# A gated-attention and mixture-of-experts layer on one core: the relative bias split into a constant on ScalarE and a short matmul part

## What is computed

```
qk  = einsum('bis,bjs->bij', q, k)
idx = arange(L)[None, :] - arange(L)[:, None] + (L - 1)        # L = 512
qk  = qk + w_rel[idx][None]                                    # w_rel has 2*128 - 1 = 255 entries
kernel = square(relu(qk / sqrt_s))
out = u * einsum('bij,bje->bie', kernel, v)
```

## Time and profile before

| | |
|---|---|
| median of 3 runs | 356.28 us (356.17 to 356.88) |
| profiled execution, its time | 356.23 us |
| profiled execution, its span | 354.2 us (2.0 us lie around it) |
| granted clock of PE, mean | 0.976 |
| PE / ACT / DVE / POOL busy | 89% / 68% / 67% / 54% of the span |
| attention stage, ticks a = 0 to 7 | about 34 to 198 us |
| expert blocks | about 201 to 341 us |

### The profile page before, as it was taken

How to read it: one execution, slowest core, us unless ns; L and a number is a source line. 1 busy time by engine, 2 the same in 40 slices (tenths; PEclk the granted TensorE clock), 3 DMA queues, 4 the chain that set the end, 5 groups by cost and what they waited for, 6 DMA issues and landing times.

```text
span 354.2 us, 7616 instructions
## 1 busy us (share of the span) xinstructions
PE 314.9 (89%) x2031; PEld 255.1 (72%) x2031; DVE 238.2 (67%) x739; ACT 239.5 (68%) x466; POOL 190.0 (54%) x193
## 2 busy tenths in 40 slices
PE   1279999999999999999996879999999999999940
PEld 1167657575756647575653779999999999999940
DVE  1578548888787778879869466785555555556843
ACT  1455948969798796979654348677777777776710
POOL 7150305136667586647658077657776455455460
PEclk9999999999999999999999699999999999999995
DMA  6983100000101010010101232323333322239518
GB/s 161 306 296 88 44 0 2 0 0 24 39 8 45 10 38 23 25 38 8 55 15 46 60 94 68 93 70 85 106 103 99 95 71 74 61 81 332 164 41 237
DMA packets 33403, 28.39 MB, mean 80 GB/s; under 512 B 5399, under 2 KB 28868, under 8 KB 33364
## 3 DMA queue, kind: packets, MB, share of 16 engines
q1 hardware_dynamic: 25634, 16.43, 16.6%
q0 software_dynamic: 4320, 8.47, 7.2%
q10 hardware_dynamic: 3410, 3.03, 3.2%
HBM read 16.75 MB, written 11.61 MB: 80 GB/s over the span
## 4 chain that ended last, share of the span: by engine, by line
PE 49%; POOL 12%; issue 12%; DVE 11%; ACT 11%; DMA 3%; SPq 1%; POOLq 0%; ACTq 0%; DVEq 0%
PE B_o L855 17%; PE B_uv L844 17%; POOL slots L455 6%; PE B_o L794 4%; ACT xs L540 2%; PE B_m L718 2%; ACT gswap L582 2%; ACT acc L540 2%; ACT s_rel L564 2%; PE B_o L785 2%; POOL rs L446 1%; DVE go L1045 1%; PE B_S L769 1%; ACT gbase L576 1%; ACT th_u L525 1%
## 5 line engine op out<-in xcount | busy, mean ns | idle before, releaser
L486 POOL DMA_INDIRECT y<-u,xb x71 | 70.4, 992 | 47.6 <-ACT u L654 37.1
L855 PE MATMUL B_o<-W2s,K 128*128 x568 | 75.3, 276 | 2.3 <-DVE K L1203 2.3
L455 POOL DMA_INDIRECT slots<-rows,pos x64 | 64.8, 1013 | 18.6 <-issue 17.3
L855 PEld LDWEIGHTS B_o<-W2s,K 128*128 128x128 f32 x568 | 69.0, 192 | 2.8 <-issue 2.7
L785 PE MATMUL B_o<-K,v 128*128 128x512 f32 x128 | 59.3, 596 | 0.0
L643 ACT ACTIVATE t<-W1s 128x644 f32 x36 | 26.6, 740 | 21.9 <-DVE yd L1209 21.3
L844 PE MATMUL B_uv<-xbT,t 128*128 128x128 f32 x288 | 38.1, 275 | 0.0
L1203 DVE TENSOR_TENSOR K<-B_uv,t 128x512 f32<-128x512 f32 x36 | 24.8, 692 | 18.4 <-PE B_uv L844 18.2
L785 PEld LDWEIGHTS B_o<-K,v 128*128 128x128 f32 x128 | 22.9, 190 | 19.8 <-issue 18.2
L844 PEld LDWEIGHTS B_uv<-xbT,t 128*128 128x128 f32 x288 | 35.1, 192 | 0.0
L773 PE MATMUL B_S<-G,ident_r 128*128 128x512 f32 x64 | 32.9, 594 | 0.0
(11 more groups left out here) (197 smaller groups left out, 653.4 us busy)
## 6 DMA issues: line engine op xcount, KB each, us to landing
xb<-slots SPq DMA_DIRECT2D x71, 65.0 KB, 1.9
x_all<-L_attn_x SPq DMA_DIRECT2D x8, 256.0 KB, 3.1
W1s<-L_ffn_W SPq DMA_DIRECT2D x1, 2048.0 KB, 11.7
x_all<-y SPq DMA_DIRECT2D x4, 512.0 KB, 6.4
out<-acc SPq DMA_DIRECT2D x6, 256.0 KB
y<-u,xb POOLq DMA_INDIRECT x71, 2.3
slots<-rows,pos POOLq DMA_INDIRECT x64, 2.4
slots<-zrow SPq DMA_DIRECT2D x9, 65.0 KB, 2.9
```

What stands on the lines that cost most here:

```text
L455: pool.indirect_dma_start(out=slots, out_offset=bass.IndirectOffsetOnAxis(ap=pos[:, q % 2, c:c + 1], axis=0), in_=rows[:, q % 2, c // T, c ...
L486: pool.indirect_dma_start(out=y2, out_offset=bass.IndirectOffsetOnAxis(ap=xb[:, k, D:D + 1].bitcast(u32), axis=0), in_=yb[:, k, :], in_off ...
L855: last = nc.tensor.matmul(B_y[n % 2], hT[:, n % 2, c * P:(c + 1) * P], W2s[:, bass.ds(w + c * D, D)], start=(c == 0), stop=(c == T - 1))
```

## The change

Three things are done. Relu takes the last entry of w_rel as a bias, one value for all partitions, read through an SBUF operand `w_last` that a new DMA on ACT's queue fills. `G` holds the bias minus that constant, 256 columns wide, and the bias matmuls run for j-tile 0 on its last 256 columns and for j-tile 1 on its last 128 alone. Everything that builds `G` shrinks accordingly: 384 entries in `w_row` and `w_long`, 256 columns in `w_skew`, two blocks in PE's `bias_window`. ACT waits for the new DMA in batch 0 and DVE in its `bias_window`. Per tick this takes 8 bias matmuls of 512 columns to 2 of 256 and 2 of 128.

```diff
--- before.py
+++ after.py
@@ -53,7 +53,7 @@
 
     slots = nc.dram_tensor("slots", [SLOTS, RW], f32).ap()
     y2 = nc.dram_tensor("y2", [ROWS * TOPK, D], f32).ap()
-    w_long = nc.dram_tensor("w_long", [1, 2 * L - 1], f32).ap()
+    w_long = nc.dram_tensor("w_long", [1, 3 * P], f32).ap()
     NREL = w_rel.shape[1]
 
     ctx = ExitStack()
@@ -93,7 +93,8 @@
         uvT = sb("uvT", [P, 2, 5 * P], f32r)
         owT = sb("owT", [P, 2, D])
 
-        G = sb("G", [P, 2, 7 * P], f32r)
+        G = sb("G", [P, 2, 2 * P], f32r)
+        w_last = sb("w_last", [P, 1])
         ident_r = sb("ident_r", [P, P], f32r)
         gb = sb("gb", [P, 2, 2])
         g_half = sb("g_half", [P, 2])
@@ -141,12 +142,12 @@
         gswap = sb("gswap", [P, 2, L])
         t1 = sb("t1", [P, 2, L])
 
-        w_row = th_u[0:1, 0:2 * L - 1]
+        w_row = th_u[0:1, 0:3 * P]
 
         t2 = sb("t2", [P, 2, L])
         qk = sb("qk", [P, 2, L])
         s_rel = sb("s_rel", [P, 2, L])
-        w_skew = s_rel[:, :, :].rearrange("p k l -> p (k l)")[:, 0:7 * P]
+        w_skew = s_rel[:, :, :].rearrange("p k l -> p (k l)")[:, 0:2 * P]
         K = sb("K", [P, T, L])
         go = sb("go", [P, 2, L])
         x1 = sb("x1", [P, T, D])
@@ -221,7 +222,7 @@
         s_ld_uvw, s_ld_b1, s_ld_small, s_ld_skew = sem("uvw_loaded"), sem("b1_loaded"), sem("small_loaded"), sem("skew_loaded")
         s_w_row, s_ld_rope, s_ld_rep, s_ld_w1 = sem("bias_row_filled"), sem("rope_loaded"), sem("rep_loaded"), sem("w1_loaded")
         s_ld_w2, s_ld_b2 = sem("w2_loaded"), sem("b2_loaded")
-        s_ld_affine = sem("ffn_affine_loaded")
+        s_ld_affine, s_ld_last = sem("ffn_affine_loaded"), sem("last_bias_loaded")
         s_pool0 = sem("pool_constants")
         s_wT_ps, s_wT = sem("weights_transposed_psum"), sem("weights_transposed")
         s_gh = sem("g_half_ready")
@@ -332,7 +333,7 @@
             sp.dma_start(sinT[:, :], rope_sin).then_inc(s_ld_rope, 16)
             sp.wait_ge(s_ld_skew, 32)
             sp.dma_start(w_skew[:, :], bass.AP(tensor=w_long.tensor, offset=0,
-                                               ap=[[1, P], [1, 7 * P]])).then_inc(s_ld_skew, 16)
+                                               ap=[[1, P], [1, 2 * P]])).then_inc(s_ld_skew, 16)
             for rep, vector in ((res_rep, res_scale), (br_rep, br)):
                 sp.dma_start(rep[:, :], vector.partition_broadcast(P)).then_inc(s_ld_rep, 16)
             load_x(2)
@@ -498,6 +499,8 @@
         def _(act):
             act.dma_start(w_row[:, 0:NREL], w_rel).then_inc(s_ld_skew, 16)
             act.dma_start(ow_raw[:, :], o_w).then_inc(s_ld_uvw, 16)
+            with nc.allow_non_contiguous_dma(reason="one word for all partitions, once"):
+                act.dma_start(w_last[:, :], w_rel[0, NREL - 1:NREL].partition_broadcast(P)).then_inc(s_ld_last, 16)
             with nc.allow_non_contiguous_dma(reason="512 words, once"):
                 for n, w in enumerate((gamma, beta)):
                     act.dma_start(gb[:, n, :], w.rearrange("k s -> s k")).then_inc(s_ld_small, 16)
@@ -561,7 +564,8 @@
 
                 act.wait_ge(s_ps, 4 * b + j + 1)
                 after(act, k_step, 8 * b + 2 * j - 2)
-                nc.scalar.activation(s_rel[:, j % 2, :], B_S[:, j % 2, :], ACT.Relu).then_inc(k_step, 1)
+                after(act, s_ld_last, 0 if b else 16)
+                nc.scalar.activation(s_rel[:, j % 2, :], B_S[:, j % 2, :], ACT.Relu, bias=w_last[:, :]).then_inc(k_step, 1)
                 if j == 0:
                     after(act, av_ps, b)
                 act.wait_ge(k_step, 8 * b + 2 * j + 1)
@@ -701,8 +705,8 @@
 
 
                 te.wait_ge(s_ld_skew, 48)
-                for s in range(7):
-                    d = 6 - s
+                for s in range(2):
+                    d = 1 - s
                     last = nc.tensor.matmul(B_o[:, s * P:(s + 1) * P], w_skew[:, d * P:(d + 1) * P], flip[:, :],
                                             start=True, stop=True)
                 last.then_inc(s_wT_ps, 1)
@@ -766,12 +770,13 @@
                 for j in range(T):
                     if not isinstance(b, int) or 4 * b + j >= 2:
                         te.wait_ge(k_step, 8 * b + 2 * j - 3)
-                    nc.tensor.matmul(B_S[:, j % 2, :], qk[:, 1, j * P:(j + 1) * P], qk[:, 0, :],
-                                     start=True, stop=False)
-
-                    for part in range(2):
-                        last = nc.tensor.matmul(B_S[:, j % 2, :], ident_r[:, :], G[:, part, (3 - j) * P:(3 - j) * P + L],
-                                                start=False, stop=(part == 1))
+                    varies = (2 - j) * P
+                    last = nc.tensor.matmul(B_S[:, j % 2, :], qk[:, 1, j * P:(j + 1) * P], qk[:, 0, :],
+                                            start=True, stop=True)
+                    if varies > 0:
+                        for part in range(2):
+                            last = nc.tensor.matmul(B_S[:, j % 2, L - varies:], ident_r[:, :], G[:, part, 0:varies],
+                                                    start=False, stop=(part == 1), skip_group_check=True)
                     last.then_inc(s_ps, 1)
 
             def attend(b, q, tiles):
@@ -945,7 +950,7 @@
             ts(selcum[:, :], ones[:, 0:NE], 0.0, None, ALU.mult).then_inc(s_dve0, 1)
 
             dve.wait_ge(s_ld_skew, 16)
-            cp(w_row[:, NREL:], w_row[:, NREL - 1:NREL].broadcast_to([1, 2 * L - 1 - NREL])).then_inc(s_w_row, 1)
+            cp(w_row[:, NREL:], w_row[:, NREL - 1:NREL].broadcast_to([1, 3 * P - NREL])).then_inc(s_w_row, 1)
 
             def small_weights():
                 dve.wait_ge(s_ld_small, 16 * 4)
@@ -972,9 +977,11 @@
             def bias_window():
                 dve.wait_ge(s_wT_ps, 2)
                 cp(ident_r[:, :], ident[:, :])
-                cp(G[:, 0, :], B_o[:, 0:7 * P]).then_inc(s_wT, 1)
+                dve.wait_ge(s_ld_last, 16)
+                ts(G[:, 0, :], B_o[:, 0:2 * P], w_last[:, :], None, ALU.subtract).then_inc(s_wT, 1)
                 dve.wait_ge(s_wT, 3)
-                tt(G[:, 1, :], B_o[:, 0:7 * P], G[:, 0, :].bitcast(f32), ALU.subtract).then_inc(s_wT, 1)
+                stt(G[:, 1, :], B_o[:, 0:2 * P], w_last[:, :], G[:, 0, :].bitcast(f32), ALU.subtract,
+                    ALU.subtract).then_inc(s_wT, 1)
 
             def ln1_stats(b):
                 link = chain(ln1_step, 3, b)
```

## The result

The changed kernel takes 360.50 us (median of 4 runs, 359.46 to 362.07) against 356.47 for the kernel before; the ratio is 1.0116, with an interval of 1.0074 to 1.0158. Measured once more on another chip it was 1.0119 (1.0083 to 1.0155), at a median of 360.84 us against 356.26. One of its six runs, 364.44 us, lies over 1.5% above its fastest; it is in that median and not in the ratio. The prediction had 357.1 us and a range up to 358.0. The direction held, the size did not: over three quarters of the loss of 4.0 us lies outside the sum of +0.9.

A forecast was written before the change was run, and what follows sets the result against it. The prediction took ACT and DVE to set the tick period, with PE close behind. Its terms, -0.30 + 0.06 + 0.04 + 0.93 + 0.2 = +0.9 us on 356.23, gave 357.1 us, range 355.4 to 358.0.

The forecast's parts named there:

- What bounds a tick: Attention ticks: ACT and DVE set the period of 20.6 us, PE is close behind, no scores matmul in the chain.
- rival 3: Attention ticks: PE was the bound after all, 1.37 us fall away in each of 7 periods, 346.6 us; chance 0.07.
- Part 2: Relu's bias operand on ACT: 0.19 us more on the period, +0.93 us over ticks 2 to 6.
- d: Extra ACT time of one Relu for its SBUF operand: taken as 93 ns, bounds 0 and 191 ns.
- rival 1: Relu on ACT: the operand is free where ACT waits anyway, d near 0, 355.5 us; chance 0.17.
- Part 3: Opening: DVE's copy filling the row shrinks from 0.45 to 0.15 us, -0.30 us; the new DMA costs nothing.
- Part 5: Ticks 0 and 1: earlier starts on ACT against four operand costs each, +0.06 and +0.04 us.
- Part 6: The end: output(7) runs at the low clock and the clock's return comes later, +0.2 us, bounds 0 and 0.3.
- Part 4: Building G in the opening: less work costs nothing, though PE then idles about 2.7 us before project_v(0).
- rival 2: Opening: the clock falls in the new gap before project_v(0), +1.5 us, 358.6 us; chance 0.08.
- Part 1: Bias matmuls in each tick: PE relieved of 1.37 us, worth nothing in the period as PE waits longer for xs.

The follow-up runs named there:

- alone-run: Changed kernel with PE's matmuls and the opening put back as in the kernel before, so only Relu's operand is new: 357.76 us, ratio 1.0038.
- e6: Kernel before with only G built the short way, scores unchanged, PE's gap before project_v(0) left open: repeat 356.71 us, ratio 1.0014.
- e7: Kernel before with G built the short way plus five unread blocks in bias_window filling PE's gap: repeat 355.20 us, ratio 0.9973.

## Why the prediction was wrong

**What bounds a tick: right.** The chain runs through ACT and DVE, and no scores matmul is in it. The period is 20.78 us for a predicted 20.8, and rival 3 is out.

**Part 2, the operand: right.** d was taken as 93 ns; the runs with none, one and two give about 90 and 86. The alone-run, which the account put at 358.0 (nothing starts earlier there), took 357.8. The changed kernel itself has 674 ns, 85 more. The point from which rival 1 decides, 41 ns, is far off.

**Part 3: right,** 0.33 us for 0.30, and the new DMA is nowhere in a chain. **Part 5: right,** ticks 0 and 1 together moved by -0.02 us for the +0.10 forecast. **Part 6: right,** 3.37 us for output(7), +0.2 as said; PE had been idle 4.18 us before the first block's transpose. The blocks' first B_o<-W2s,K starts another 0.1 us later that no term has.

**Part 4, the lost cover: the first failed step.** The gap of 2.55 us was weighed between one of 1.86 that did no harm and one of almost 3.5 that did, and the sum took the harmless side, with 0.08 for rival 2. The clock fell there in all six profiles with the short build and no filling, after gaps of 2.09 to 2.88 us, and in none with a gap of 1.92 or less. In the run with the short matmuls alone it fell 1.2 us after project_v(0) had begun. Rival 2's 1.5 us is what it cost (1.54 in the trace, 1.5 between the medians of e6 and e7). The prediction also misread its citation: the warning of the Trainium skill, page TensorE: Matmul & The Clock Gate, section "Why this matters for your kernels", is for gaps somewhat longer than this one, so it did not put the cost of rival 2 into the sum. What decides here are the traces: the clock at 0.50 from 24 us on.

**Part 1, "in the period this is worth nothing, since PE only waits longer for xs": the second failed step,** and one that no rival covered. The size was right: from the start of the scores to that of project_u PE takes 3.90 us in tick 4 (118.24 to 122.14) for 5.29 before (116.69 to 121.98), 1.39 less for the 1.37 forecast. The split of a j-tile behind that forecast, 0.86 us for q and k and 0.46 for the bias matmuls, does not come out of the starts in the earlier trace rows, which would give 0.46 and 0.86; it stands in the chain of waits (0.86 at 37.07 us, 0.46 at 37.92), and the 1.39 bears it out. The edit was costed at nothing with ACT as the cover, but the bias matmuls had themselves kept up the clock. The work taken from PE became 0.9 to 1.24 us of idle time before the router, and the 0.48 before the transposes stayed, with only eight matmuls of 8 columns in between; the prediction had expected one wait of 1.9 us for xs. In ticks where the clock then fell, attend of the last tile and the first part of project_v ran at half the rate behind xs, where PE has nearly no slack, and such a tick lost 1.1 to 1.4 us. I weighed idle time and clock for the one long gap and not for the ticks. The profiles show one or two such falls between 40 and 190 us. The median stands 3.4 us above the sum, and 1.9 above the sum with rival 2 in it (358.6).

With both terms the sum is 357.1 + 1.5 = 358.6, and with one or two falls in the ticks at 1.4 each 360.0 to 361.4; the measurement is 360.5. What decides in which tick of which execution the clock falls stays open.

## What to carry to other kernels

Removing work from TensorE is not free of effect, even where it is not the bound: where PE stands close behind the engine that bounds, the removed matmuls can have been what kept its clock up. Before costing such an edit at nothing, list PE's waits after the edit, small matmuls between them counted as little, and price what follows each of them at half the clock. If a fall shows, matmuls that nobody reads, put ahead of the wait into a free half of PSUM, can hold the clock: five in each tick bought 2.2 us here, and 3.4 with those of the opening and of tick 0, and the period of a tick stayed as it was. A per-partition operand of an ACT instruction in the chain costs 90 ns each time.

## What was not expected of the hardware

- The clock fell after two waits of 1.24 and 0.48 us with small matmuls between them, and in other executions after 0.90 and 0.48, where 1.25 us in the same execution did nothing; I had looked only for a single gap.
- The same wait (1.01 us at 45 to 47 us) is followed by a fall in some executions and not in others, and one fall costs 1.1 to 1.5 us. The runs of the changed kernel spread over 2.6 us in the first measurement and 6.5 in the second, while kernels with all gaps filled stay within 0.7 to 1.6 us, as the kernel before does (0.7 to 1.6).
- On the chip where all ran near 388 us, the clock fell in a tick of e7 as well, at 111.5 us, and in two of e6, at 112.4 and 156.7, with the full bias matmuls on PE; before each of them PE had waited 0.67 to 0.69 us and then 0.48. The kernel before may stand closer to such falls than its own profile shows; no trace of it on that chip was kept.
